# Results written over the split x, x loads before the stores, gathers spread, and zero products on TensorE

## The reference, cut to what matters

```python
Bx   = einsum('bni,bri->bnr', x, B[ids]);  c = einsum('bnr,bor->bno', Bx, A[ids])
y    = einsum('bth,oh->bto', c, W) + b
z    = einsum('bth,erh->bter', c, lora_A); alpha = softmax(c @ router_W.T ...)
x    = x + y + einsum('bteo,bte->bto', einsum('bter,eor->bteo', z, lora_B) * 2, alpha)
```

## Time and profile before

| what | us |
|---|---|
| median of 3 runs | 379.61 |
| lowest and highest run | 379.27 and 385.32 |
| the profiled execution | 380.75 |
| span of its trace | 379.1 |

### The profile page before, as it was taken

One profiled execution on the slowest core, in us unless ns is written; L12 is line 12 of the kernel. 1 busy time (PEld: TensorE's weight loads), 2 busy tenths in 40 slices (PEclk: granted clock), 3 DMA queues, 4 the chain that ended last, 5 costly groups with the idle time before them and its releaser, 6 DMA issues.

```text
span 379.1 us, 6637 instructions
## 1 busy us (share of the span) xinstructions
PE 318.2 (84%) x1960; PEld 300.0 (79%) x1960; DVE 245.9 (65%) x470; ACT 146.6 (39%) x300; POOL 116.1 (31%) x126
## 2 busy tenths in 40 slices
PE   0946573979996899969996999699969999899785
PEld 0945473968995799969996999699968898889684
DVE  5916961688675676666675669476847875784535
ACT  5848531383052515351354216530634064502300
POOL 0024640064035601641075206430455026502100
PEclk9968858699999699979998799989996999899969
DMA  7898799600798058904893279517970698043605
GB/s 278 305 311 286 241 173 250 220 0 21 223 300 178 1 153 269 284 19 129 279 265 46 82 245 286 107 33 247 290 150 6 223 302 188 1 165 99 72 0 221
DMA packets 33830, 65.87 MB, mean 174 GB/s; under 512 B 4881, under 2 KB 22162, under 8 KB 32658
## 3 DMA queue, kind: packets, MB, share of 16 engines
q1 hardware_dynamic: 31762, 57.25, 47.7%
q0 software_dynamic: 2048, 8.39, 12.6%
HBM read 47.80 MB, written 17.83 MB: 173 GB/s over the span
## 4 chain that ended last, share of the span: by engine, by line
PE 34%; DMA 27%; issue 10%; POOL 8%; DVE 7%; SPq 7%; ACT 4%; POOLq 0%; ACTq 0%
DMA out<-xraw 12%; DMA xraw<-x_in 10%; PE ps_d L327 6%; PE ps_d L328 5%; PE ps_d L329 5%; POOL xs_lo L919 5%; DMA xraw<-w 5%; PE ps_d L520 4%; SPq L239 3%; SPq L241 3%; PE ps_p L327 2%; PE ps_h L334 2%; POOL a1s_lo L919 2%; PE ps_p L328 2%; PE ps_p L329 2%
## 5 line engine op out<-in xcount | busy, mean ns | idle before, releaser
L919 POOL TENSOR_TENSOR xs_lo<-xraw,xs_hi 128x512 fp32r<-128x512 f32 x48 | 62.9, 1315 | 94.9 <-ACT xs_hi L530 94.9
L327 PE MATMUL ps_d<-w1s_hi,a1s_hi 128*128 128x384 f32 (+1 forms) x216 | 75.1, 348 | 14.9 <-DVE w1s_lo L692 14.9
L329 PE MATMUL ps_d<-w1s_hi,a1s_lo 128*128 128x384 f32 (+1 forms) x216 | 72.5, 335 | 0.0
L328 PE MATMUL ps_d<-w1s_lo,a1s_hi 128*128 128x384 f32 (+1 forms) x216 | 72.5, 335 | 0.0
L944 POOL DMA_DIRECT2D res<-m_tab x64 | 31.5, 496 | 120.7 <-PE ps_d L329 118.3
L327 PE MATMUL ps_p<-xs_hi,bst_hi 128*128 128x256 f32 x128 | 44.3, 346 | 22.5 <-POOL xs_lo L919 15.3
L327 PEld LDWEIGHTS ps_d<-w1s_hi,a1s_hi 128*128 128x128 f32 x216 | 43.5, 201 | 15.6 <-issue 8.8
L905 DVE SCALAR_TENSOR_TENSOR xraw<-ps_d,bsum,xraw 128x512 f32<-128x512 f32 x62 | 45.0, 747 | 13.2 <-PE ps_d L520 13.2
L530 ACT ACTIVATE xs_hi<-xraw 128x512 fp32r<-128x512 f32 x64 | 38.3, 627 | 37.2 <-DMA xraw<-x_in 36.6
L327 PEld LDWEIGHTS ps_p<-xs_hi,bst_hi 128*128 128x128 f32 x128 | 30.6, 239 | 25.9 <-POOL xs_lo L919 17.1
L328 PEld LDWEIGHTS ps_d<-w1s_lo,a1s_hi 128*128 128x128 f32 x216 | 43.4, 201 | 0.0
(11 more groups left out here) (143 smaller groups left out, 658.5 us busy)
## 6 DMA issues: line engine op xcount, KB each, us to landing
xraw<-x_in SPq DMA_DIRECT2D x32, 512.0 KB, 6.2
out<-xraw SPq DMA_DIRECT2D x32, 512.0 KB, 3.6
xraw<-w SPq DMA_DIRECT2D x16, 512.0 KB, 6.3
abraw<-ab_tab SPq DMA_DIRECT2D x64, 128.0 KB, 2.1
res<-m_tab POOLq DMA_DIRECT2D x64, 128.0 KB, 5.8
b0raw<-b_tab SPq DMA_DIRECT2D x64, 64.0 KB, 1.9
m_tab<-res SPq DMA_DIRECT2D x1, 1024.0 KB, 6.4
b0raw<-a SPq DMA_DIRECT2D x1, 512.0 KB, 3.7
```

Of the source, the lines that this page charges most:

```text
L327: pe.matmul(acc, lh, rh, start=first, stop=False, skip_group_check=True)
L328: pe.matmul(acc, lh, rl, start=False, stop=False, skip_group_check=True)
L329: return pe.matmul(acc, ll, rh, start=False, stop=final, skip_group_check=True)
L919: return pool.tensor_tensor(dst, whole, high.bitcast(F32), ALU.subtract)
```

## The change

1. `done`, a view of the memory of `xs_hi` and `xs_lo` (16 KB a partition). The results of a step go there and no longer over `xraw`; the stores read it. ACT's first-half split of chunks into `xs_hi` waits for `stored[0]` or `stored[1]` of the step before, POOL's into `xs_lo` for `stored[2]` or `stored[3]`.
2. SP loads chunk i of x(g + 2) as soon as the two result tiles are made, ahead of the store of chunk i, and waits for no store.
3. Four sequences are gathered ahead of the first chunk, one ahead of each of chunks 1, 2 and 3, and the last behind chunk 3.
4. In steps after the first, `split_b(g + 1)` stands behind the first softmax on ACT and DVE, and `coef_high(0)`/`coef_low(0)` ahead of the parts of wide(1).
5. TensorE makes products whose operand is zero (`stay_busy`, 128x512 each, into the unused `ps_z`): 18 at its start, behind a wait for `init_done`, 18 behind the products of W0, 12 behind the transposes, 8 behind the projections of step 0.

```diff
--- before.py
+++ after.py
@@ -91,7 +91,10 @@
         xraw = [sb(f"xraw{i}", [P, KT, TOK]) for i in range(2)]
 
         slots = [t[:, KC * i:KC * (i + 1), :].rearrange("p k t -> p (k t)") for t in xraw for i in range(CH)]
+        xs_at = nc.sbuf_base
         xs = split("xs", [P, KT, HALF])
+
+        done_ = nc.alloc_sbuf_tensor_at("done", [P, KT * TOK], F32, offset=xs_at)
         abraw = sb("abraw", [P, GROUP, 2, SLOT])
         b0raw = sb("b0raw", [P, GROUP, SLOT])
         bst = split("bst", [P, KT, 4, HR_])
@@ -128,6 +131,7 @@
         bsum = sb("bsum", [P, KT])
 
         hr_hi, hr_lo = hr[:, :, 0, :], hr[:, :, 1, :]
+        done = [done_[:, KC * TOK * i:KC * TOK * (i + 1)] for i in range(CH)]
         exp1_hi, exp1_lo = (w[:, :, D:WIDE] for w in w1s)
 
         m0_tab = nc.dram_tensor("m0_tab", (ADAPT0, RANK, 2, D), F32)
@@ -209,6 +213,10 @@
         def result_banks(last):
 
             return ps_d + [ps_p, ps_h] if last else ps_d
+
+        def stored_by(g):
+
+            return 0 if isinstance(g, int) and g == 0 else 16 * g - 16
 
         def after_step(eng, signal, count):
 
@@ -301,18 +309,17 @@
                 if ahead:
                     picks = pick(g + 2)
                     sp.wait_ge(a_lo, g + 2)
-                    gather(picks, range(GROUP))
+                    gather(picks, range(HSEQ))
                 for i in range(CH):
+                    if ahead and i > 0:
+                        gather(picks, range(HSEQ - 1 + i, HSEQ + i))
                     sp.wait_ge(d_out, KT * g + KC * (i + 1))
+                    if ahead:
+                        load_x(g + 2, par, i)
                     sp.dma_start(out[bass.ds(g, 1), :, KC * i:KC * (i + 1), :]
-                                 .rearrange("a p k t -> p (a k) t"),
-                                 xraw[par][:, KC * i:KC * (i + 1), :]).then_inc(stored[i], 16)
-                    if ahead and i > 0:
-                        sp.wait_ge(stored[i - 1], 16 * g + 16)
-                        load_x(g + 2, par, i - 1)
+                                 .rearrange("a p k t -> p (a k t)"), done[i]).then_inc(stored[i], 16)
                 if ahead:
-                    sp.wait_ge(stored[CH - 1], 16 * g + 16)
-                    load_x(g + 2, par, CH - 1)
+                    gather(picks, range(GROUP - 1, GROUP))
 
             steps(sp, body, 3)
             for i in range(CH):
@@ -368,12 +375,20 @@
                     mm.then_inc(x_used, 1)
 
 
+            def stay_busy(count):
+
+                for _ in range(count):
+                    pe.matmul(ps_z[:], hle[:, 0, :], ce[:], start=True, stop=True, skip_group_check=True)
+
+            pe.wait_ge(init_done, 1)
+            stay_busy(18)
             pe.wait_ge(a0_lo, 1)
             for k in range(KT):
                 pe.wait_ge(w0_lo, k + 1)
                 for n in (0, 2):
                     mm = wide_product(n, a0s, w0s, k)
             mm.then_inc(m0_done, 1)
+            stay_busy(18)
 
             pe.wait_ge(m0_copy, 2)
             pe.wait_ge(ident_in, 16)
@@ -392,8 +407,10 @@
             for k in (6, 7):
                 mm = turn_m0(k)
             mm.then_inc(m0t_done, 1)
+            stay_busy(12)
             project(0, 0)
             project(0, 1)
+            stay_busy(8)
             pe.wait_ge(m0t_lo, 2)
             pe.wait_ge(small_lo, 5)
             pe.wait_ge(init_done, 1)
@@ -535,6 +552,8 @@
                     act.wait_ge(x_in_sem[i], 16 * g + 16)
                     if not (isinstance(n, int) and n == 0):
                         act.wait_ge(x_used, CH * n + (i + 1 - CH))
+                    if half == 0:
+                        after_step(act, stored[i // KC], stored_by(g))
                     copy(xs[0][:, KC * i:KC * (i + 1), :],
                          xraw[par][:, KC * i:KC * (i + 1), half * HALF:(half + 1) * HALF]).then_inc(x_hi, 1)
 
@@ -624,8 +643,6 @@
                 first = isinstance(g, int) and g == 0
                 if not first:
                     h_and_k1(g)
-                if not last and not first:
-                    split_b(g + 1)
 
                 def wide_high(n):
                     cols, at = WIDE_PARTS[n]
@@ -657,8 +674,13 @@
                 softmax_exp(0)
                 if first:
                     experts_high()
-                wide_high(1)
-                coef_high(0)
+                    wide_high(1)
+                    coef_high(0)
+                else:
+                    if not last:
+                        split_b(g + 1)
+                    coef_high(0)
+                    wide_high(1)
                 if first:
                     split_x(g + 1, 1 - par, 0, [0])
                     split_b(g + 1)
@@ -870,8 +890,13 @@
                 softmax(0)
                 if first:
                     experts_low()
-                wide_low(1)
-                coef_low(0)
+                    wide_low(1)
+                    coef_low(0)
+                else:
+                    if not last:
+                        split_b(g + 1)
+                    coef_low(0)
+                    wide_low(1)
                 if first:
                     split_b(g + 1)
 
@@ -901,8 +926,11 @@
                 banks = result_banks(last)
 
                 for m in range(KT):
+                    if last and m % KC == 0:
+                        dve.wait_ge(stored[m // KC], 16 * g)
                     dve.wait_ge(d_done, KT * g + m + 1)
-                    dve.scalar_tensor_tensor(out=xraw[par][:, m, :], in0=banks[m % len(banks)][:],
+                    dve.scalar_tensor_tensor(out=done[m // KC][:, m % KC * TOK:(m % KC + 1) * TOK],
+                                             in0=banks[m % len(banks)][:],
                                              scalar=bsum[:, m:m + 1], in1=xraw[par][:, m, :],
                                              op0=ALU.add, op1=ALU.add).then_inc(d_out, 1)
                     if not last and m == 1:
@@ -921,6 +949,8 @@
             def split_x(g, par, half, chunks):
                 for i in chunks:
                     pool.wait_ge(x_hi, 2 * CH * g + CH * half + i + 1)
+                    if half == 0:
+                        after_step(pool, stored[KC + i // KC], stored_by(g))
                     low(xs[1][:, KC * i:KC * (i + 1), :],
                         xraw[par][:, KC * i:KC * (i + 1), half * HALF:(half + 1) * HALF],
                         xs[0][:, KC * i:KC * (i + 1), :]).then_inc(x_lo, 1)
```

## The result

| kernel | median us | lowest and highest | ratio to before, 95% interval |
|---|---|---|---|
| before | 379.44 (4 runs) | 377.15 to 385.32 | |
| changed | 395.14 (4 runs) | 390.94 to 398.04 | 1.0324, 1.0219 to 1.0428 |

The change makes the kernel 3.2% slower by the ratio, 4.1% by the medians. 367.6 was forecast, in a range of 356 to 382; the time lies outside it. The two spans differ by 10.2 us, of the 12.2 between the changed kernel's quick runs and the median of before.

The account below looks back on a forecast made before the run. The loop was taken as bound by TensorE's work plus one late transfer a step; 24 us saved over six steps less 12 us lost in the prologue took 379.6 to 367.6 us, range 356 to 382.

Parts of the forecast that it names:

- What bounds the loop: Steps 1 to 6: TensorE's work plus one late transfer a step; 39.96 us a step to become 36.0.
- The step without waits: Loop step 2 with its two waits and the clock loss taken off: 40.03 - 2.09 - 0.95 - 3.1 = 33.9 us.
- the 0.95 of the earlier trace: TensorE's idle before layer 1's routing products, waiting for DVE's `cf`; kept in the forecast as 1.0 us a step.
- The prologue: Start through step 0: zero products behind `init_done` make it 12 us later, bounds 8 and 15.
- When the last gather lands: In SP's queue: 10.4 us into the step if nothing else runs, 12 to 13.5 with POOL's copies.
- Its price: TensorE waiting on the b split: each us of gather lateness costs one; 1.0 us taken, bounds 0 and 3.5.
- the fall of the clock: TensorE's clock at 0.50 within a step: 3.1 us loss to go, 0.1 a step still charged.
- rival B: Loop: gathers land late and the clock falls, 40 us a step, no gain, 391 us; chance 0.12.
- a 1.0 for `cf`: TensorE's wait for DVE's `cf` before layer 1's routing products, charged at 1.0 us a step.
- The b split: ACT and DVE behind the first softmax: `l_lo` just in time without lateness, TensorE asking 16.5 us into the step.
- The new waits for `stored`: POOL's splits of x waiting for stores: no cost, up to 1 us if the queue is slower.
- Rival C: Prologue costs less (8 us) and the loop reaches 35 us a step: 357 us; chance 0.17.

Follow-up runs that it names:

- e2: The changed kernel with all 16 gathers ahead of the first load, zero products kept: 376.69 us, ratio 1.0117 to before.
- e1: The changed kernel without any zero product or TensorE's wait for `init_done`, all else kept: 380.45 us, ratio 1.0108 to before.
- e3: The changed kernel without zero products and with all gathers ahead of the first load: 364.45 us, ratio 0.9608 to before.
- e8: e4 with only TensorE's wait for `init_done` at its start kept, no zero products: 365.12 us, ratio 0.9683 to before.
- e5: e4 with all four groups of zero products, the first started by the memset of the zeros: 359.67 us, ratio 0.9600 to before.
- e11: e1 with POOL's eight copies bringing 1 row instead of 16 from step 1 on: 363.4 us, ratio 0.9561 to before.
- e4: e3 with the b split back in its old place ahead of the first softmax: 360.28 us, ratio 0.9496 to before.
- e12: e1 (gathers spread) with the b split back in its old place ahead of the first softmax: 419.8 us, ratio 1.1044 to before.
- e9: e4 with the middle quarters of `done` exchanged, so POOL's first split waits for store 1: 358.61 us, ratio 0.9456 to before.
- e7: e4 with the four loads of x ahead of all four stores: 379.49 us, ratio 1.0083 to before.

## Why the prediction was wrong, point by point

- **What bounds the loop.** Right: TensorE's work plus one late transfer. The step without waits that the sum started from, 33.9, is borne out: steps 3 and 6 of e2, in which TensorE waits nowhere for more than 0.5 us, take 34.1. The chunk of x was early in the changed kernel (ACT waits for `x_in` once in the run, 3.5 us), and the 0.95 of the earlier trace rows shrank with it.
- **The prologue.** Right, the terms within 1 us. ACT took up the first part of W0's product at 34.08 (33.1 was worked out, plus its own start), the F part at 42.09 (41.3), the transposes began at 37.99 (37.3); 12.4 us in all against 12. e1 and e3 take it away again, e8 and e5 show that it was the place and not the products.
- **When the last gather lands: the step that failed.** The working had 14 us of queue time from 3.6 ahead of the step, so 10.4, and 12 to 13.5 with POOL's copies. It was 15.4 to 17.5, 16.5 on average. The term that was mis-sized is the 14 us. In e11, almost without the copies, the gathers landed at 14.1 instead of 10.4. Its step 3 shows 17.2 us from the first load to ACT going on, and 5.2 MB moved in them, which is 13.9 us at 373 GB/s. The middle 12 us ran as the working had it (369). By these rows, as an estimate, 1.6 us were lost ahead of the step (201 GB/s) and 1.5 at the end, where little but the last gathers was left. At the start stand the gathers still on their way and a slow issue by SP; how the loss divides between them, and what holds the tail, stays open. The copies were charged with 1.6 to 3.1; the changed kernel against e11 has 2.5, so that term was right.
- **Its price.** "Each us that a gather is late is a us of TensorE" was right: in all six steps TensorE asked for `ce` 16.6 to 16.8 us in (16.5 was worked out) and got it 3.9 us behind ACT's start (3.4 to 4.3). So the waits are 2.6 to 4.7 where 1.0 was taken, with bounds of 0 and 3.5. This idle time then brought back the fall of the clock, 3.4 to 6.8 us at 0.50 in each step, where 0.1 was charged: 39.8 a step less 34.1 of work and 3.8 of wait leaves 1.9, an estimate of what it costs. That is rival B: 40 us a step, no gain, 391. The trace has 39.8 and 390.94. B had a chance of 0.12. Its mechanism came true. That its number came so near is in part luck: it had 3.5 of waiting and 1.6 of clock for 3.8 and 1.9, and a 1.0 for `cf`, of which the changed kernel's list shows next to nothing in the loop, makes up for it.
- **The b split.** Costed at nothing but its lateness. With the gathers in time (e3 against e4) the move costs 4 us by the medians, and saves nothing; it serves only to soften part 3 (e12).
- **The new waits for `stored`.** Costed at none. In the changed kernel so (POOL 3.2 us, off the path). With the gathers first, where the six steps are shorter, POOL waits 17.6 to 24.4 us for stores (e2, e3, e4, e9), and e9 shows that some of it reaches TensorE.
- **The chances.** The mechanism of B was worked out and given 0.12; a bound of 3.5 for the lateness was in the text, but the value taken was 1.0, from a queue that runs at its full rate from the first load to the last gather. The rate of one stretch of 2 us was used for the whole; it held for 12 us and not ahead of them and behind them.
- **A slip.** Rival C puts the prologue at 8 but adds 7 in its sum; with 8 it comes to 358. It changes nothing here.

By the Trainium skill, page "DMA: Bandwidth & Descriptors", section "Queues, rings and completion order", each engine takes turns between the queue rows it has work for. e11 is in line with it: the last gathers, at the tail of SP's row, landed 2.5 us earlier than in the changed kernel with 0.98 MB less in POOL's. It does not show in what order the engines took the packets.

## What to carry to other kernels

When transfers are reordered in one queue, write down for each the time at which its reader needs it and the time at which it can land, with the issuing engine's own pace and the other queues in the sum: the gain of the ones put forward is paid by the last one. A move of a consumer to fit a late transfer is worth only what the lateness was; undo both and measure. Filler products on TensorE are free only where it would have stood anyway, so look at what the semaphore they wait for comes behind.

## What the runs showed of the hardware

- A `DMA_DIRECT2D` on SP takes 0.33 us to issue at the start of a burst, and single ones in a burst of gathers and 512 KB transfers take up to 1.28 us in the changed kernel, 1.57 in e4 and 2.17 in e7. So SP gets through such a burst more slowly than the count of its issues says.
- Loads, stores and some gathers in SP's queue ran at 369 to 374 GB/s for 12 us in the changed kernel and e11, and at 201 to 208 in the 3.5 us before, when gathers made up much of what was in flight.
- In the middle of each step of the changed kernel the clock fell to 0.50 behind idle times of 2.6 to 4.7 us and came back after 3.4 or 6.8 us; in e11 it stood at 1.00 over six steps in which TensorE idled 0.6 to 2.5 us once a step. In the earlier trace rows the fall came behind 1.19 and 0.94 close together. How long a single idle time was does not by itself decide it.
